# The staircase by destination and the weight loads, moved into the ranking block

## The reference

```python
edge_index = jnp.stack([src, dst])
x = _layernorm(x + _L0_gnn_ref(x, edge_index, edge_weight), axis=-1)      # exp(-w) * x[dst], summed by src
x = _layernorm(x + _L1_gnn_ref(x, edge_attr_32, edge_index, ...), axis=-1) # attention with 4 heads, by dst
x = _layernorm(x + _L2_gnn_ref(x, edge_index, W_l, W_r, att, bias), axis=-1) # GATv2, by dst
x = _layernorm(x + _L3_gnn_ref(x, edge_index, W1, b1, W2, b2), axis=-1)    # two mean-aggregating layers, by src
```

## Time and profile before

| what | value |
|---|---|
| runs of the kernel before | 4355.29, 4366.24, 4365.61 us (median 4365.61) |
| the profiled execution | 4373.95 us |
| its span, first to last instruction | 4372.3 us |
| busy in the span: PE, PEld, DVE, ACT, POOL | 2241.3, 1689.7, 2245.4, 666.9, 2579.3 us |
| mean granted clock of TensorE | 0.613 of full speed |

### The profile page before, as it was taken

How to read it: one execution, slowest core, us unless ns; L and a number is a source line. 1 busy time by engine, 2 the same in 40 slices (tenths; PEclk the granted TensorE clock), 3 DMA queues, 4 the chain that set the end, 5 groups by cost and what they waited for, 6 DMA issues and landing times. The chain is left out here.

```text
span 4372.3 us, 79196 instructions
## 1 busy us (share of the span) xinstructions
PE 2241.3 (51%) x19380; PEld 1689.7 (39%) x19381; DVE 2245.4 (51%) x4750; ACT 666.9 (15%) x1478; POOL 2579.3 (59%) x2627
## 2 busy tenths in 40 slices
PE   3343333333325542555555555436666666664997
PEld 1333333233324432444444444324444444442332
DVE  5532111121137745666666666647777777777001
ACT  0011111111124410111111111101111111111000
POOL 0477777777742215777777777137777777772000
PEclk8555555555555555666666666556666766765999
DMA  1453334343346645666666666135555555553954
GB/s 38 149 136 128 126 124 131 116 135 122 107 115 193 194 48 145 171 171 166 171 169 171 170 170 170 29 75 153 154 152 155 155 150 158 155 151 80 337 183 145
DMA packets 641999, 630.49 MB, mean 144 GB/s; under 512 B 127546, under 2 KB 472794, under 8 KB 641856
## 3 DMA queue, kind: packets, MB, share of 16 engines
q1 hardware_dynamic: 356958, 357.61, 27.4%
q0 software_dynamic: 89104, 141.91, 13.9%
q10 hardware_dynamic: 195858, 130.02, 9.8%
HBM read 444.40 MB, written 186.44 MB: 144 GB/s over the span
## 5 line engine op out<-in xcount | busy, mean ns | idle before, releaser
L1537 POOL DMA_INDIRECT rows<-nodes_xl,id_slot x832 | 821.1, 987 | 394.6 <-issue 248.9
L1537 POOL DMA_INDIRECT rows<-nodes_kv,id_slot x832 | 831.1, 999 | 319.8 <-issue 248.3
L826 POOL DMA_INDIRECT msg_by_src<-message,place_slot x832 | 833.1, 1001 | 264.3 <-issue 253.1
L779 PE MATMUL picked<-X,hotT 128*128 x1664 | 373.2, 423 | 636.3 <-issue 361.7
L779 PEld LDWEIGHTS picked<-X,hotT 128*128 128x128 f32 x1664 | 360.2, 331 | 650.6 <-issue 650.6
L1936 PE MATMUL sums<-parts,hot 128*128 128x68 bf16 (+1 forms) x4992 | 325.6, 251 | 383.9 <-DVE parts L1717 383.9
L1733 DVE SCALAR_TENSOR_TENSOR running_counts<-running_counts,same_block,counts_p 128x128 f32<-128x128 f32 x1040 | 357.5, 344 | 278.6 <-PE counts_p L1892 170.0
L734 DVE TENSOR_TENSOR message<-picked,w_dst 128x512 f32<-128x512 f32 x104 | 71.9, 691 | 790.6 <-ACT message L799 756.4
L1936 PEld LDWEIGHTS sums<-parts,hot 128*128 128x128 bf16 x4992 | 312.1, 167 | 405.4 <-issue 405.4
L1892 PE MATMUL counts_p<-hot_src,hot_blocks 128*128 128x128 bf16 x2080 | 247.3, 277 | 222.4 <-DVE running_counts L1733 220.8
L1892 PEld LDWEIGHTS counts_p<-hot_src,hot_blocks 128*128 128x128 bf16 x2080 | 196.0, 155 | 259.4 <-DVE running_counts L1733 233.1
(11 more groups left out here) (402 smaller groups left out, 3656.4 us busy)
## 6 DMA issues: line engine op xcount, KB each, us to landing
hot_src<-hot_src_by_cell SPq DMA_DIRECT2D x1040, 64.0 KB
adjacency<-running_counts ACTq DMA_DIRECT2D x1040, 64.0 KB
loc_all<-loc_by_cell SPq DMA_DIRECT2D x104, 512.0 KB
hotT<-hotT_by_step SPq DMA_DIRECT2D x208, 256.0 KB
hot<-hot_by_step SPq DMA_DIRECT2D x208, 256.0 KB
blocks<-adjacency SPq DMA_DIRECT2D x40, 1280.0 KB
hot_by_step<-hot ACTq DMA_DIRECT2D x104, 256.0 KB, 2.0
hotT_by_step<-hotT ACTq DMA_DIRECT2D x104, 256.0 KB, 2.2
```

Source lines behind the costliest of these rows:

```text
L779: ins = nc.tensor.matmul(picked[:, s, 2 * q + g, :], hotT[:, s, 2 * q + g, :], X[:, bass.ds(n, 1), :].rearrange("p a c -> p (a c)"), start ...
L826: pool.indirect_dma_start(out=msg_dram, out_offset=bass.IndirectOffsetOnAxis(ap=ids[:, s, t:t + 1], axis=0), in_=rows[:, s, t, :], in_offs ...
L1537: pool.indirect_dma_start(out=rows[:, j, t, :], out_offset=None, in_=table, in_offset=bass.IndirectOffsetOnAxis(ap=ids[:, j, t:t + 1], axis=0)
```

## The change

The two blocks `load_weights` and `staircase` are gone. Their work stands inside the block of `rank`, which now takes the list of small loads as an argument.

The keys come no longer from the stored records but straight from the input `dst`, as integers, by four DMAs of GpSimd; this saves one cast. On VectorE the first half of the staircase (to the first diagonals) stands between the tile shift and the copy of the transposed tiles, the second half between the 25 compares and the scan, and the copy to `n_all` behind the split in bytes. On TensorE the two multiplications by ones stand ahead of the counts and behind them, in the second half of `place_p`. ScalarE issues the 17 loads behind its copy of the sources. SyncE writes and reads back the cell lists ahead of its wait for the finished records. The diff, without declarations of tiles and semaphores:

```diff
-        def rank():
+        def rank(small):
...
+                pB, pN = place_p[:, 1, 0:CB * P], place_p[:, 1, 512:512 + CB * P]
...
                     @block.sync
...
+                        sp.wait_ge(k_made, 1)
+                        with nc.allow_non_contiguous_dma(reason="one word of each cell"):
+                            sp.dma_start(k_dram["dst"].rearrange("(b p) -> p b", p=P), k_i[:]).then_inc(put, 16)
+                            sp.dma_start(n_dram["dst"].rearrange("(b p) -> p b", p=P), n_i[:]).then_inc(put, 16)
+                        sp.wait_ge(put, 32)
+                        sp.dma_start(k_row["dst"][:], k_dram["dst"][0:CELLS].rearrange("(a k) -> a k", a=1)).then_inc(back, 16)
+                        sp.dma_start(n_row["dst"][:, BODY:], n_dram["dst"][0:CELLS].rearrange("(a k) -> a k", a=1)).then_inc(back, 16)
                         sp.wait_ge(filled, 1)
...
                         sp.wait_ge(stored, 32)
+                        sp.wait_ge(back, 32)
+
+                    @block.gpsimd
+                    def _(pool):
+                        nc.gpsimd.iota(kk[:], [[1, CB * P]], base=0, channel_multiplier=0,
+                                       allow_small_or_imprecise_dtypes=True).then_inc(iotas, 1)
+                        nc.gpsimd.iota(cell[:], [[P, CB]], base=0, channel_multiplier=1,
+                                       allow_small_or_imprecise_dtypes=True).then_inc(iotas, 1)
+                        pool.wait_ge(keys_clear, 1)
+                        keys = dst.rearrange("(k e) -> k e", e=GROUP)[:, GROUP - 1:GROUP]
+                        with nc.allow_non_contiguous_dma(reason="one key of each group"):
+                            for b in range(CB):
+                                m = P if b < full_b else rest_b
+                                pool.dma_start(last_i[:m, b:b + 1], keys[b * P:b * P + m, :]).then_inc(keys_in, 16)
 
                     @block.scalar
...
                         nc.scalar.copy(rec[:, :, :, 0], s_i[:]).then_inc(kept, 1)
+                        for to, frm in small:
+                            act.dma_start(to, frm).then_inc(small_in, 16)
                         act.wait_ge(loaded[1], 32)
                         nc.scalar.copy(rec[:, :, :, 1], d_i[:]).then_inc(kept, 1)
                         act.wait_ge(loaded[2], 32)
                         nc.scalar.activation(rec[:, :, :, 2], w_f[:], ACT.Exp, scale=-1.0).then_inc(ew, 1)
+                        act.wait_ge(small_in, 16 * len(small))
 
                     @block.vector
...
+                        v.memset(last_i[:], 0).then_inc(keys_clear, 1)
...
                         v.tensor_copy(tile_f[:], tile_i[:]).then_inc(tiled, 1)
+                        dve.wait_ge(keys_clear, 1)
+                        dve.wait_ge(keys_in, 16 * CB)
+                        stairs(v.tensor_single_scalar(last_i[:], last_i[:], 7, op=ALU.arith_shift_right))
+                        stairs(v.tensor_copy(last[:], last_i[:]))
+                        for b in range(CB):
+                            ins = v.tensor_scalar(diag[:, b, :], ident[:], last[:, b:b + 1], None, ALU.mult)
+                        ins.then_inc(diag_made, 1)
                         dve.wait_ge(turned, 1)
                         step(v.tensor_copy(tile[:], place_p[:, 0, 0:CHUNK]))
                         for t in range(NT):
                             v.tensor_scalar(hit[:, t, :], tile[:], float(t), None, ALU.is_equal).then_inc(hits, 1)
 
+                        dve.wait_ge(iotas, 2)
+                        dve.wait_ge(keys_spread, 1)
+                        stairs(v.tensor_tensor(group_ends[:], pB, kk[:], ALU.add))
+                        stairs(v.memset(group_ends[:, GROUPS:], 1.0e6))
+                        for b in range(CB):
+                            stairs(v.tensor_scalar(less[:], group_ends[:], cell[:, b:b + 1], None, ALU.is_lt))
+                            stairs(v.tensor_reduce(k_f[:, b:b + 1], less[:], AX.X, ALU.add))
+                        stairs(v.tensor_scalar(k_f[:], k_f[:], float(GROUPS - 1), None, ALU.min))
+                        stairs(v.tensor_tensor(n_f[:], cell[:], k_f[:], ALU.subtract))
+                        stairs(v.tensor_scalar(n_low[:], n_f[:], float(NT - 1), None, ALU.min))
+                        stairs(v.tensor_copy(n_i[:], n_low[:]))
+                        stairs(v.tensor_copy(k_i[:], k_f[:]))
+                        stairs(v.tensor_scalar(n_f[:], n_f[:], float(P), None, ALU.mult))
+                        for b in range(CB):
+                            ins = v.tensor_scalar(diag[:, b, :], ident[:], n_f[:, b:b + 1], None, ALU.mult)
+                        ins.then_inc(k_made, 1)
                         dve.wait_ge(counted, 1)
...
                         v.tensor_copy(bytes_h[:], bytes_i[:]).then_inc(split, 1)
+                        dve.wait_ge(n_spread, 1)
+                        v.tensor_copy(n_all[:], pN[:, 0:CELLS]).then_inc(n_copied, 1)
 
                     @block.tensor
...
                         ins.then_inc(turned, 1)
+                        pe.wait_ge(diag_made, 1)
+                        nc.tensor.matmul(pB, ones[:], diag[:].rearrange("p b q -> p (b q)"), start=True, stop=True).then_inc(keys_spread, 1)
                         for t in range(NT):
                             pe.wait_ge(hits, t + 1)
...
                         ins.then_inc(counted, 1)
+                        pe.wait_ge(k_made, 1)
+                        nc.tensor.matmul(pN, ones[:], diag[:].rearrange("p b q -> p (b q)"), start=True, stop=True).then_inc(n_spread, 1)
                         pe.wait_ge(totals, 1)
...
                         for t in range(NT):
                             if t >= 2:
                                 pe.wait_ge(placed, t - 1)
+                            if t == 1:
+                                pe.wait_ge(n_copied, 1)
...
-        def staircase(keys):
...
-        def load_weights(X, pairs):
...
         setup()
-        load_weights(X, [(wq_s, wqkv), (bq_s, bc(bqkv)), (weT_s, weT), (be_s, bc(be)), (lt_s, bc(log_temp)), (wo_s, woT),
...
-        rank()
-        staircase(rec_dram.rearrange("(k e) r -> k (e r)", e=GROUP)[:, GROUP * REC - REC + 1:GROUP * REC - REC + 2])
+        rank([(X[:], x.rearrange("(t p) d -> p t d", p=P))] + [(to[:], frm) for to, frm in (
...
```

More of the change, by code:

```diff
@@ L207, in rank @@
                 place_p = psum("place_p", [P, 2, 2 * 512], r)
+                last_i = sbuf("last_i", [P, CB], I32, ctx=r)
+                last = sbuf("last_tile", [P, CB], ctx=r)
+                diag = sbuf("diag", [P, CB, P], ctx=r)
+                group_ends = sbuf("group_ends", [P, CB * P], ctx=r)
+                kk = sbuf("kk", [P, CB * P], ctx=r)
+                less = sbuf("less", [P, CB * P], ctx=r)
+                cell = sbuf("cell", [P, CB], ctx=r)
+                n_low = sbuf("n_low", [P, CB], ctx=r)
+                n_i = sbuf("n_i", [P, CB], I32, ctx=r)
+                pB, pN = place_p[:, 1, 0:CB * P], place_p[:, 1, 512:512 + CB * P]
+                full_b = GROUPS // P
+                rest_b = GROUPS - full_b * P
                 PIECES = [(0, 512), (512, CHUNK)]
@@ L214, in rank @@
                     cleared, tiled, turned, turned_back, filled = (sem(n, r) for n in ("cleared", "tiled", "tiles_turned", "turned_back", "filled"))
+                    keys_clear, keys_in, iotas, diag_made, keys_spread, k_made, n_spread, n_copied, put, back, small_in, own_k = (
+                        sem(n, r) for n in ("keys_clear", "keys_in", "iotas", "diag_made", "keys_spread", "k_made", "n_spread", "n_copied",
+                                            "put", "back", "small_in", "own_stairs"))
                     @block.sync
@@ L246, in _ @@
                         v = nc.vector
+                        stairs = serial(dve, own_k)
+                        v.memset(last_i[:], 0).then_inc(keys_clear, 1)
                         for to in (s_i, d_i, w_f):
@@ L2082, in _ @@
                         sp.wait_ge(s, 16)
-        def load_weights(X, pairs):
-            with ExitStack() as c, nc.Block() as block:
-                s = sem("weights_in", c)
-                @block.sync
-                def _(sp):
-                    sp.dma_start(X[:], x.rearrange("(t p) d -> p t d", p=P)).then_inc(s, 16)
-                    for to, frm in pairs:
-                        sp.dma_start(to[:], frm).then_inc(s, 16)
-                    sp.wait_ge(s, 16 * (len(pairs) + 1))
         nodes_dram = {k: dram(f"nodes_{k}", [NPAD, w]) for k, w in (("kv", 2 * D + HEADS), ("xl", D + 2))}
```

85 lines of the change are left out of this document (3 added, 82 removed).

## The result

The changed kernel takes 4388.18 us (median of 5 runs, 4383.82 to 4393.24) against 4365.61 (5 runs, 4355.29 to 4370.23): ratio 1.0048, 95% interval 1.0034 to 1.0061. It is slower by half a per cent, where I had forecast 1% faster, and 52 us above the upper end of my range. The profiled execution took 4388.18 us with a span of 4386.5, 14.2 us longer than that of before, which lay 8.3 us above its median.

The account below looks back on a forecast made before the run. It took the load and staircase blocks as paid in full, in series with the unchanged rest: -14.45 - 36.14 + 4.05 + 1.4 = -45.1 us, from the median 4365.6 to 4320.5 us, range 4306 to 4336.

Parts of the forecast that it names:

- (a): Load block, from its first issue to the ranking's first issue, barrier included: goes away, 14.45 us saved.
- (d): Ahead of ranking's compares: VectorE waits for the last keys, a delay of 1.4 us (bounds 0 and 12).
- (c): Staircase's second half on VectorE, between compares and scan: 8.03 us, partly in an idle hole, making the scan 4.05 us late.
- The covers: Work costed at nothing as hidden, including small loads (11.2 us uncovered) and SyncE's staircase chain (some 18 us of room).
- The sum: All terms together, two blocks removed less what returns in ranking: 45.1 us less, next block starting that much earlier.
- Rival 1: Ranking's keys come late because GpSimd can't write descriptors while VectorE works: delay 6.2 us, time 4325.3; chance 0.10.
- Rival 2: SyncE's staircase word writes come late and delay the record store: at three times their 17.9 us, 4338; chance 0.03.
- Rival 3: Long loops run slower through TensorE's granted clock: at a mean of 0.61, time 4385; chance 0.03.
- Rival 4: The change doesn't shorten the way, as the next block's start waits for something else: time 4365; chance 0.02.
- the first part: Opening account of what bounds the kernel: two blocks are paid in full, and the rest of the span is untouched.

Follow-up runs that it names:

- nine fillers: Changed kernel plus nine semaphore increments nobody waits for, at the head of VectorE's stream; 4332.2 us against 4372.2 before, ratio 0.991.
- 24 and 119 fillers: Kernel before plus 24 or 119 semaphore increments nobody waits for, on VectorE in the load block; 4398.59 us (ratio 1.0068) and 4437.92 us (1.0142).
- the staircase alone: Kernel before with only the staircase moved into ranking, keys by GpSimd, five extra VectorE increments, load block kept; 5822.21 us against 5856.36, ratio 0.9934.

## Why the prediction was wrong

**What held.** Every point up to the loops came in:

- (a) The load block: first issue of the ranking at 2.49, forecast 2.5.
- (d) The keys' wait: 1.56 us of it is seen at the shift, and the tile copy starts at 11.43, which is 1.06 behind 24.82 - 14.45 = 10.37; forecast 1.4. The two parts were sized otherwise, though: an issue took 2.34 / 4 = 0.58 us and not 1.24, and the landing was the longer part.
- (c) and (d) together: the scan at 27.22, 4.92 behind 36.75 - 14.45 = 22.30, directly behind the diagonals; forecast 5.45.
- The covers. The 17 issues took 12.5 us on ScalarE's queue, and the exponential, over at 22.49, is 44 us ahead of the store. SyncE read the lists back at 44.47, 22 us ahead of the store at 66.88. `n_all` fits ahead of the first predicated copy. The first two steps take 2.60 us together, as before.
- The sum: the gather at 74.70, forecast 119.89 - 45.1 = 74.79.

**The rivals.** Rival 1 falls by its size: it wanted a delay of 6.2 us, and 1.06 were measured. GpSimd's issues weren't held by a VectorE at work, with four in 2.34 us from 3.13 on. That the landing took 4.8 us has little to do with who issued, for SyncE's four, a little later in the same block, took 4.0 (8.25 to 12.24). By the Trainium skill ("SBUF — State Buffer", the box on how DVE blocks a software-generated DMA) GpSimd can't write descriptors while VectorE is in a two-port mode; this trace shows no such delay, but it doesn't show either which of VectorE's instructions were in that mode. And the 832 issues that I had cited against the rival were not all "beside a working VectorE": VectorE is busy 249 us of that loop's 1085.5. Rival 2 falls by the 22 us. Rival 3 had the sign and, by luck, nearly the number (at 0.61, 4385), by a mechanism that wasn't at work: the granted clock of the GAT stage did fall, from 0.67 to 0.65, but nine fillers brought it back without moving the stage. TensorE waited more, and its clock followed. Rival 4 falls by the gather at 74.70. (The upper end of the range, 4336, is 4333.6 by its own terms; that changes nothing.)

**The step that failed** is a sentence of the first part: the rest of the span "is not touched by the diff; it starts earlier or later, and is otherwise the same work." Same work it was, and not the same time. Two terms were missing that I had set to nothing without a row:

- The place of code: +47.1 us in the stage and +5.9 behind it. The stretch behind goes with the place in every kernel profiled on the faster chips: 407.8 us here, 406.7 and 408.3 with 24 and 119 fillers in the kernel before, but 401.9 to 402.8 in the five whose body stays loaded. VectorE is further behind GpSimd when the gathers end: from the last gather to the stage's last `total` on VectorE it takes 43.8 us here and 38.4 before, 5.4 of the 5.9.
- GpSimd's key loads: +6.7 us in the message loop, shown by their removal (1085.1 us without them, against 1092.2 and 1091.8). I had asked when they would land, and not what they would leave behind.

-45.1 + 47.1 + 5.9 + 6.7 = +14.6, and the spans differ by 14.2. What was there before held the warning in part: a loop of 364 instructions in the built program, and in the trace 12 packets on q14 in a stage of 13 passes, so the body stayed loaded. It couldn't show how near it was to not staying. What I inferred from all the placements: a body that touches three pieces stays, and one that touches four is fetched anew, five packets a pass. For VectorE's 364 instructions three are touched from 21 of 128 places and four from all others; 1473 and 1601 hold, 1464, 1497 and 1592 don't. The second wait bounds where the edges lie. In the built program `running_counts` is the body's 7th instruction and `score_a` its 10th; the one runs at once and the other waits, so, if an instruction runs only once its piece is there, from 1464 and from 1592 an edge comes 7 to 9 instructions into the body, at 1471 to 1473 and every 128 from there. That gives all five placements as they were found. From 1497 the first edge comes over 100 instructions into the body, and there is one wait a turn and not two. For SyncE's 314 in attention the places 604 and 595 hold, and 573, 577 and 582 don't. With VectorE's edges 577 would touch three pieces and hold; so the rule fits SyncE only if its edges lie elsewhere, one of them somewhere from 583 to 595, and for SyncE it stays a guess.

The Trainium skill ("Runtime: NRT & Kernel Launch", section "Instruction fetch mechanics") has the rule that should have been a rival: "A taken branch whose target isn't in the current 2-page window forces a DMA fetch of the target page before execution can continue". The stall at the loop's turn, 2.56 us with a packet in it, agrees with that. The pages there are of 16 KiB, 256 instructions; q14's packets here are of 8192 bytes, and places that lie 9 below and 24 above a good one are both bad, which two pages of 256 would not give for a body of 364.

**Still open:** what the four loads do to GpSimd's later issues.

## What to carry to other kernels

Any edit ahead of a long loop moves the loop's code, so compare the packets on the instruction queue in the same stage of both kernels, and look at the first instructions behind the loop's turn for idle time that waits for nothing, or is put down to an engine that the same instruction doesn't wait for elsewhere. If the count has jumped, a few instructions that do nothing, ahead of the loop on the engine that others wait for, tell in one run whether the place is the cause; here nine of them turned +0.5% into -0.9%, and on the slower chips they did no harm (0.9917 against 0.9925). An early, short piece of work on the engine that paces a later loop can also lengthen each of that loop's issues, as it did in one of three loops here; compare the issue times of a loop before and after.

## What the runs showed of the hardware

- Code comes in packets of 8192 bytes on q14 (and of 16384 on q8). A loop body of 364 instructions that sits badly is fetched in five packets per pass and holds VectorE 2.6 us at the turn. With the first edge 7 to 9 instructions into the body it is held once more, 1.8 to 1.9 us on average. In a stage of 1073.6 us this costs 25 us with one wait a turn, 47 to 52 with two. New fetches in attention's stage, most likely SyncE's (314 instructions), cost nothing measurable.
- Four direct loads of single words by GpSimd at the start made each of 832 later indirect DMAs of one loop some 9 ns longer (974 to 983), and none if SyncE issued them.
- GpSimd's issues of such loads took 0.58 us each, and landed 4.8 us behind the end of the last issue (5.47 to 10.2); SyncE's four behind the input arrays took 0.48 each (1.90 / 4), landed 4.0 us behind (8.25 to 12.24) and were awaited 3.06 us.
- The same kernel takes 4366 to 4377 us on some chips and 5824 to 5859 on others. In the kernel with 119 fillers, profiled on both kinds, 1389 of 1408 us of difference lie in the three loops of gathers and scatters (the GAT stage moves 154 GB/s in the kernel before on the one kind, 91 in that with the staircase alone on the other), and stalls that cost 1.4% on the one kind cost 0.1 to 0.4% on the other.
